# Attention into experts: where block 3's root, the gates, the shared matmuls and the late rows stand

## The reference, cut to what matters

```
x = x + tanh(g_xattn[1]) * _L1_xattn_ref(_layernorm(x), ctx, ...)
x = x + tanh(g_ffn[1])   * _L1_ffn_ref(_layernorm(x), gate, ...)

scores = sigmoid(xt @ gate.T)
_, sel = top_k(scores + expert_bias, 2)        # two experts for a row
xb = (xt[token] * score).astype(bfloat16)
for e in range(8):
    h = silu(xb @ w1e.T) * (xb @ w3e.T);  oe = h @ w2e.T     # added where expert == e
hs = silu(xt @ shared_w1.T) * (xt @ shared_w3.T)
out = hs @ shared_w2.T + the experts' rows
```

## Time and profile before

| what | value |
|---|---|
| time, median of 3 runs | 217.3 us (217.23 to 218.14) |
| the profiled execution's own time | 218.29 us |
| its span | 216.5 us, 3594 instructions |
| TensorE busy (matmuls) | 177.0 us, 82% |
| VectorE busy | 163.7 us, 76% |
| ScalarE busy | 106.9 us, 49% |
| POOL busy | 84.6 us, 39% |
| share of the chain that ended last: PE, DVE, ACT | 50%, 21%, 10% |

### The profile page before, as it was taken

One profiled execution on the slowest core, in us unless ns is written; L12 is line 12 of the kernel. 1 busy time (PEld: TensorE's weight loads), 2 busy tenths in 40 slices (PEclk: granted clock), 3 DMA queues, 4 the chain that ended last, 5 costly groups with the idle time before them and its releaser, 6 DMA issues.

```text
span 216.5 us, 3594 instructions
## 1 busy us (share of the span) xinstructions
PE 177.0 (82%) x1156; PEld 112.2 (52%) x1156; DVE 163.7 (76%) x465; ACT 106.9 (49%) x280; POOL 84.6 (39%) x123
## 2 busy tenths in 40 slices
PE   0369999999989989886789788888889568989992
PEld 0236555567555556543356465556666126744651
DVE  0798989995177899988688999999946942475854
ACT  2440243111423244641568798898877641554441
POOL 1385558016655550493032204222221396039000
PEclk9999999999999999997579999999999876999999
DMA  6989970000000000000000000000000245639862
GB/s 175 400 218 374 359 255 15 3 0 0 0 0 2 3 0 2 0 0 2 3 0 0 5 0 5 0 3 0 3 0 3 50 93 101 76 72 170 164 152 97
DMA packets 22625, 15.17 MB, mean 70 GB/s; under 512 B 17648, under 2 KB 21328, under 8 KB 22096
## 3 DMA queue, kind: packets, MB, share of 16 engines
q1 hardware_dynamic: 21968, 13.94, 24.3%
q10 hardware_dynamic: 640, 1.02, 1.3%
HBM read 9.68 MB, written 1.07 MB: 50 GB/s over the span
## 4 chain that ended last, share of the span: by engine, by line
PE 50%; DVE 21%; ACT 10%; issue 8%; DMA 6%; POOL 3%; SPq 0%; DVEq 0%
PE PS L1668 6%; PE PS L1334 5%; PE PS L1336 5%; PE PS L1335 5%; PE PS L1686 5%; DMA X<-x 4%; PE PS L1422 4%; PE PS L1398 3%; PE PS L1356 3%; ACT R L668 3%; ACT R L663 2%; PE PS L1498 2%; PE PS L1365 2%; DVE T_R L974 2%; POOL R L507 2%
## 5 line engine op out<-in xcount | busy, mean ns | idle before, releaser
L507 POOL TENSOR_SCALAR R<-QT,SM 128x256 bf16<-128x256 f32 x32 | 16.1, 520 | 15.6 <-DVE SM L1117 15.3
L1284 DVE TENSOR_TENSOR R<-R,PS 128x512 bf16<-128x512 f32 (+1 forms) x17 | 11.5, 683 | 13.7 <-PE PS L1668 7.3
L1036 DVE TENSOR_REDUCE SM<-PS 128x8 f32<-128x1024 f32 x16 | 18.8, 1213 | 3.7 <-PE PS L1498 2.5
L1512 PE MATMUL PS<-CON,R 128*128 128x128 f32 x128 | 19.0, 281 | 1.2 <-ACT R L668 1.2
L476 POOL TENSOR_TENSOR R<-R,CON 128x256 f32<-128x256 f32 x16 | 9.6, 620 | 25.3 <-PE PS L1498 16.2
L668 ACT ACTIVATE R<-PS 128x512 f32<-128x512 f32 x32 | 18.4, 601 | 1.2 <-PE PS L1512 1.0
L1686 PE MATMUL PS<-R 128*128 128x256 bf16 (+1 forms) x80 | 15.3, 318 | 4.3 <-DVE R L1284 4.0
L341 POOL TENSOR_TENSOR R<-CT 128x512 f32<-128x512 f32 x12 | 13.4, 1113 | 13.2 <-PE PS L1336 8.0
L1668 PE MATMUL PS<-R 128*128 128x512 bf16 x64 | 16.8, 382 | 0.1
L1512 PEld LDWEIGHTS PS<-CON,R 128*128 128x128 f32 x128 | 14.5, 143 | 3.5 <-issue 3.0
L790 ACT ACTIVATE R<-PS 128x512 f32<-128x512 f32 x17 | 10.1, 595 | 11.4 <-PE PS L1668 11.2
(11 more groups left out here) (155 smaller groups left out, 432.7 us busy)
## 6 DMA issues: line engine op xcount, KB each, us to landing
WST<-w SPq DMA_DIRECT2D x3, 1024.0 KB, 11.3
T_R<-lagged SPq DMA_DIRECT2D x2, 768.0 KB, 8.0
X<-x SPq DMA_DIRECT2D x2, 512.0 KB, 6.8
CT<-ctxr SPq DMA_DIRECT2D x1, 1024.0 KB, 7.4
y<-X SPq DMA_DIRECT2D x8, 128.0 KB, 1.8
WKV<-wkv SPq DMA_DIRECT2D x1, 512.0 KB, 9.8
WQP<-wqp ACTq DMA_DIRECT2D x1, 512.0 KB, 6.4
R<-sw SPq DMA_DIRECT2D x3, 128.0 KB, 4.4
```

The lines of the kernel that those rows point to most:

```text
L507: nc.gpsimd.tensor_scalar(XB[:, u % XS, j, :], MX[:, b, :], GG[:, b, e:e + 1], 1.0, ALU.mult, ALU.mult).then_inc(e_xb, 1)
L1036: V_.tensor_reduce(MX1[:, b % 2, 8 * c:8 * c + 8], S4[:, 8 * c:8 * c + 8, :], AX.X, ALU.max, negate=True).then_inc(a_mx, 1)
L1512: ins = TR(PS[:, 4 + k % 2, P * h:P * h + P], SS[:, b % 2, 4 * k + h, :], I)
```

## The change

The change alters only the order of calls, in six places.

- The root of block 3 (`m_rstd(NB - 5)`) moves from the tail into the loop's last turn on ScalarE, ahead of `o_y_(4)`. Two of the four blocks' logits are made in TensorE's last loop turn.
- Block 3's transpose, its copy and the other two blocks' logits come ahead of block 7's values.
- On VectorE the six steps of the gates come right behind block 6's division, ahead of block 7's; `finish(5)` goes behind `m_rows(4)`, into block 7's division.
- Both shared hidden matmuls of group 0 come ahead of block 7's `o_transpose`.
- The late rows: `m_rows`, transposes and copies of blocks 5 to 7, and `finish(7)` with its statistics, go behind units v = 0, 1 and 2; on POOL `late_rstd` of blocks 5 to 7 moves one or more units later.
- Group 1's gates come one unit later (GE_AT 4 to 5), and ROWS_AT with them.

```diff
@@ -46,7 +46,7 @@
 NS = 14
 RING = 6
 XS = 8
-ROWS_AT = {1: (4,), 2: (5,), 3: (6,), 4: (7,), 6: (8, 9), 7: (10,), 8: (11,), 9: (12, 13), 10: (14,), 11: (15,)}
+ROWS_AT = {1: (4,), 2: (5,), 3: (6,), 4: (7,), 7: (8, 9), 8: (10,), 9: (11, 12), 10: (13,), 11: (14,), 12: (15,)}
 
 D_AT, BIAS_AT = 0, NH0
 BV_AT = BIAS_AT + NR
@@ -366,7 +366,7 @@
 
             return PS[:, ((0, 1), (6, 0))[g][j // 2], DM * (j % 2):DM * (j % 2) + DM]
 
-        GE_AT = 4
+        GE_AT = 5
 
         LOG = 512 - GT * NE
         TC = [0, 2, 4, 10, NH0]
@@ -541,13 +541,14 @@
                 finish(b)
             late_rstd(GT)
             expert_rows(0)
-            late_rstd(GT + 1)
             expert_rows(1)
             expert_rows(2)
+            late_rstd(GT + 1)
+            expert_rows(3)
             late_rstd(GT + 2)
-            expert_rows(3)
+            expert_rows(4)
             late_rstd(GT + 3)
-            for u in range(4, NG * NE):
+            for u in range(5, NG * NE):
                 expert_rows(u)
 
         @block.scalar
@@ -764,6 +765,8 @@
                     o_ev_(s - 3)
                 if s + 3 < NB:
                     a_zq_(s + 3)
+                if s == NB - 1:
+                    m_rstd(NB - 5)
                 if s >= 3:
                     o_y_(s - 3)
                 if s >= 1:
@@ -791,29 +794,27 @@
 
 
             a_exp(NB - 1, 0)
-            m_rstd(NB - 5)
             o_q_(NB - 3)
             a_exp(NB - 1, 1)
+            m_zt_(NB - 5)
             a_exp(NB - 1, 2)
             o_ev_(NB - 3)
-            m_zt_(NB - 5)
             a_exp(NB - 1, 3)
+            m_ge_(0)
             o_q_(NB - 2)
             o_y_(NB - 3)
             o_pe_(NB - 1)
-            m_ge_(0)
             o_ev_(NB - 2)
+            last_rows(0)
+            nc.scalar.preload_act_table_set("silu_and_others")
             o_y_(NB - 2)
-            nc.scalar.preload_act_table_set("silu_and_others")
-            last_rows(0)
+            last_rows(1)
+            silu(0)
             o_q_(NB - 1)
-            last_rows(1)
+            last_rows(2)
             o_ev_(NB - 1)
-            silu(0)
+            m_zt_(NB - 4)
             o_y_(NB - 1)
-            m_zt_(NB - 4)
-            last_rows(2)
-            m_zt_(NB - 3)
             last_rows(3)
 
 
@@ -823,8 +824,8 @@
                     m_ge_(1)
                 for u in ROWS_AT.get(v, ()):
                     last_rows(u)
-                if v in (1, 2):
-                    m_zt_(NB - 3 + v)
+                if v in (1, 2, 3):
+                    m_zt_(NB - 4 + v)
             v = UNITS - 1
             act.wait_ge(e_h, 2 * v + 1)
             act.wait_ge(e_ht, v - 1)
@@ -1233,32 +1234,24 @@
             m_stats(NB - 4, 1)
             for k in range(3, 6):
                 o_norm(NB - 2, k)
+            for k in range(6):
+                m_gates(0, k)
+            third_rows(0)
+            o_norm(NB - 1, 0)
+            o_norm(NB - 1, 1)
+            m_rows(NB - 4)
+            o_norm(NB - 1, 2)
             finish(NB - 3)
-            m_rows(NB - 4)
-            for k in range(4):
-                m_gates(0, k)
-            o_norm(NB - 1, 0)
-            m_gates(0, 4)
-            o_norm(NB - 1, 1)
-            m_gates(0, 5)
-            o_norm(NB - 1, 2)
-            third_rows(0)
             for k in range(3, 6):
                 o_norm(NB - 1, k)
             third_rows(1)
             m_stats(NB - 3, 0)
+            third_rows(2)
+            m_stats(NB - 3, 1)
             finish(NB - 2)
-            m_stats(NB - 3, 1)
             m_stats(NB - 2, 0)
+            third_rows(3)
             m_stats(NB - 2, 1)
-            third_rows(2)
-            m_rows(NB - 3)
-            third_rows(3)
-            finish(NB - 1)
-            m_stats(NB - 1, 0)
-            m_stats(NB - 1, 1)
-            m_rows(NB - 2)
-            m_rows(NB - 1)
 
 
             for v in range(UNITS):
@@ -1282,6 +1275,13 @@
                     dve.wait_ge(e_acc, v - 1)
                 dst = HT[:, v % 2, :] if e >= 1 else HST
                 V_.tensor_tensor(dst, HS[:, v % 2, :], PS[:, 3 + 2 * (v % 2), :], ALU.mult).then_inc(e_ht, 1)
+                if v == 0:
+                    m_rows(NB - 3)
+                    finish(NB - 1)
+                    m_stats(NB - 1, 0)
+                    m_stats(NB - 1, 1)
+                if v in (1, 2):
+                    m_rows(NB - 3 + v)
 
                 if v == GE_AT + 1:
                     for k in range(4):
@@ -1635,6 +1635,8 @@
                     a_turn(s - 1, 3)
                 if s + 1 < NB:
                     a_scores(s + 1)
+                if s == NB - 1:
+                    m_logits(0, 0, 2)
                 if s >= 3:
                     o_transpose(s - 3)
                 if s >= 1:
@@ -1698,25 +1700,23 @@
             a_turn(NB - 1, 0)
             a_turn(NB - 1, 1)
             o_rows(NB - 2)
-            m_logits(0, 0, GT - 1)
+            m_transpose(NB - 5)
+            a_turn(NB - 1, 2)
             o_transpose(NB - 3)
-            a_turn(NB - 1, 2)
-            m_transpose(NB - 5)
             a_turn(NB - 1, 3)
+            m_logits(0, 2, GT)
             o_project(NB - 3)
             for k in (0, 2, 1, 3):
                 a_values(NB - 1, k)
-            m_logits(0, GT - 1, GT)
             o_transpose(NB - 2)
             o_rows(NB - 1)
             o_project(NB - 2)
             e_hidden(0, 0)
+            e_hidden(0, 1)
             o_transpose(NB - 1)
+            m_transpose(NB - 4)
             o_project(NB - 1)
-            e_hidden(0, 1)
-            m_transpose(NB - 4)
             e_hidden(1, 0)
-            m_transpose(NB - 3)
             e_hidden(1, 1)
             for v in range(1, UNITS + 1):
                 if v < UNITS:
@@ -1724,8 +1724,8 @@
                         e_hidden(v, 0)
                         e_hidden(v, 1)
                 e_out(v - 1)
-                if v in (1, 2):
-                    m_transpose(NB - 3 + v)
+                if v in (1, 2, 3):
+                    m_transpose(NB - 4 + v)
                 if v == GE_AT - 1:
                     m_logits(1, 0, GT)
```

## The result

| kernel | runs | median, us | lowest to highest |
|---|---|---|---|
| before | 4 | 217.72 | 217.23 to 218.56 |
| changed | 4 | 208.74 | 207.89 to 209.84 |

What follows compares the result with a forecast made beforehand. TensorE was the engine to follow, with three large holes and low clock behind two. Terms 6.8 + 1.36 + 1.7 - 0.55 + 0.45 = 9.75, less 0.35, gave 9.4 us: 217.3 to 207.9 us, 8-in-10 range 206.7 to 211.0.

Steps and rivals of the forecast that it cites:

- hole 3: TensorE idle 1.29 us ahead of e_out(7), from group 1's gates; moving them one unit later gains 1.7 us.
- unit 8: Expert 8's rows on POOL come late behind the moved gates, DMA landing 190.4, wanted 189.85: gives back 0.55 us.
- The loop: Last turn: eight logit matmuls ahead of o_transpose(4) cost 0 to 0.1 us; block 3's root makes o_y(4) 0.15 late.
- Up to the shared matmuls: Tail: block 3's root no longer holds back m_rows(3); hidden(0,0) starts at 166.45 against 166.69.
- Gates and division: VectorE starts gates at 163.95; block 7's scaling ends 5.1 us later, at 169.0 instead of 170.2.
- hole 1: TensorE idle 2.13 us ahead of block 7's output transposes (170.70), low clock behind it; both predicted gone.
- First product: VectorE's first product of hidden rows starts at 171.8; e_out(0) at about 172.6 against 179.40, 6.8 us earlier.
- (a): Rival: TensorE's clock falls once more between 169.9 and 172.6, +1.7 us and more; 209.6 to 210.5, chance 0.17.
- (d): Rival, slower: clock at 1.2 GHz from the shared matmuls (166.45) on, all units at double time; some 219, chance 0.03.
- (b): Rival: the gates' hole only moves, to late rows of unit 8 and unit 5 or 6; 209.4, chance 0.14.
- (c): Rival: VectorE's queue is longer, stretched by POOL writing rows; product 0 at 173.5, 209, chance 0.10.
- (e): Rival: m_transpose(3)'s chain ends last, gates start at 166.5 as before, only 5 us won; 212.3, chance 0.04.

Runs made afterwards that it cites:

- r6: The changed kernel with block 3's root (Ln, Exp) back in the tail behind exp(7,0): 209.44 us, 0.9655 of before.
- r5: The changed kernel with m_rows of blocks 5 to 7, finish(7) and its statistics back ahead of product 0 on VectorE: 215.34 us, 0.9940 of before.
- r3: The changed kernel with block 7's output transposes and projection back between the two shared hidden halves: 211.2 us, 0.9714 of before.
- r9: The kernel before with 8 and 10 unused fp32 matmuls in TensorE's holes ahead of block 7's output transposes and e_out(0): 216.53 us, 0.9977 of before.
- r1: The changed kernel run again without an edit: 209.42 us, 0.9619 of before.
- r2: The changed kernel with group 1's gates back at their old unit (GE_AT 4, old ROWS_AT): 210.59 us, 0.9677 of before.
- r12: The kernel before with only group 1's gates one unit later (GE_AT 5, new ROWS_AT): 216.4 us, 0.9958 of before.
- r7: The kernel before with 16 and 22 unused fp32 matmuls in TensorE's holes ahead of block 7's output transposes and e_out(0): 218.14 us, 1.0049 of before.

## Why the prediction was right

By its own terms, in the profiled executions, all times from TensorE's timeline:

| term of the sum | predicted, us | measured, us | from |
|---|---|---|---|
| e_out(0) earlier | 6.8 | 6.65 | 179.40, 172.75 |
| e_out(0) to hidden(5) | 1.36 | 1.20 | 9.29, 8.09 |
| hidden(5) to hidden(9), hole 3 | 1.7 | 1.19 | 6.92, 5.73 |
| hidden(9) to hidden(11), unit 8 | -0.1 | -0.60 | 6.93, 7.53 |
| hidden(11) to the end | 0 | 0.06 | 13.96, 13.90 |
| taken off for unit 8's landing | -0.35 | in the -0.60 | |
| sum | 9.4 | 8.5 | 216.5, 208.0 |

The mechanism held in each of the four large terms, and three sizes were off. The 9.46 us of the prediction are one: they take e_out(0)'s start from the timeline and hidden(5)'s (188.86) from the chain, which puts the same matmuls 0.17 us later than the timeline does (188.69). The two others are hole 3 and unit 8, below.

- *The loop.* o_project(4) at 158.16 and o_y(4) at 158.69, 0.06 later than before, where I had taken 0.15. Nothing was lost to the eight logit matmuls, as the hole of 0.87 at that place had said.
- *Up to the shared matmuls.* They start at 166.00; predicted 166.45. The last four logits ran at 162.38, where I had 162.8, so the replay was late by 0.4 already there. The root's part is 0.76 us (r6), all of the earlier start against before.
- *Gates and division.* First step 163.68 (163.95), last 165.64, ahead of block 7's division. The scaling ends at 169.54, where I had 169.0: from the first gate step 5.86 us for 5.1, the largest miss of the replay. In it stand m_rows(4), which takes 0.58 us for 0.41, and finish(5), with POOL writing rows beside them from 165.93; no run tells whether POOL is the reason. TensorE did not wait for it, as both shared halves lasted to 169.5; of the 2.13 us of hole 1, 0.44 stayed.
- *First product.* At 172.04 (171.8); e_out(0) at 172.75 (172.6) behind a hole of 0.70 (0.7), and 1.99 us long (1.75). That it comes so close is in part luck: VectorE needed 8.36 us from the first gate step to the product, where I had 7.87, and the gates were 0.27 early. r5 shows that this term hangs on the late rows, r3 that it hangs on the shared matmuls' place too, and r9 that in the old order it did not hang on the clock behind hole 1.
- *Hole 3.* The mechanism was right: the gates' wait is the same 1.72 us and is covered. The term came out as 1.19 because hidden(6) came 0.50 late, a wait for a DMA (0.34) that r1 doesn't have.
- *Unit 8* is the mis-sized term: I had 0.55 lost, it was a wait of 0.89. The chain of waits in the changed kernel shows the parts:

```profile
188.06 0.05 POOL R L507
188.10 3.35 DMA R<-R
```

  POOL began at 186.96 instead of 186.2. That is 0.76 later, of which hidden(9) shared 0.62 (186.57 for 185.95). Then it took 1.10 for the first unit's rows, where I had taken the mean of fifteen, 0.95: the first pass alone lasts 0.64 us, as it does in the trace of before (at 193.00), and the median one 0.48. The landing of 3.35 was as predicted. A mean over a long run was the wrong row for its first unit.

*The rivals.* (a), the clock falling once more, is out: 1.00 from 160 to 192 us in the windows, behind holes of 0.44, 0.24 and 0.70. What (a) and (d) say of the trace of before, two low stretches, each behind a hole of over 2 us, misses a third: the clock is at 0.50 from 101 to 110 us as well, behind no such hole (last section), and the chances given for the clock were not worked out with it. (b), the gates' hole only moves: r2 and r12 show that the move gains 1.3 and 0.9 us net of unit 8's wait; but the half of (b) that unit 8 gives back more than I took was true. (c), product 0 at 173.5: it came at 172.04, though VectorE's queue was longer than I thought, by 0.5 us. (d) and (e) are out, by the clock and by the gates at 163.68. The rule on the table load (2.66 us by the Trainium skill, ScalarE: Activation LUTs, "What ACT_TABLE_LOAD costs") would have had e_out(0) at 173.1. In the changed kernel's timeline of ScalarE the load and its neighbours are:

```profile
165.87 0.51 ACT L786 ACTIVATE R<-QT,SM 128x256 bf16<-128x256 f32 x1 [0.35 <-DVE SM L1118]
166.39 1.28 ACT L809 ACT_TABLE_LOAD   x1
167.69 0.47 ACT L688 ACTIVATE T_R<-PS,SM 128x256 f32<-128x256 f32 x1
```

From the end of the one ACTIVATE (166.38) to the start of the next (167.69) it is 1.31 us, with work ready on both sides. The load itself is as long there as the Trainium skill gives it (1.28 us), but the trace shows no drain of 1.38 us beside it, and the sum did well to go by the row.

*The parts do not add up.* Taken back singly they cost 6.7 (late rows), 2.8 (shared matmuls), 2.0 (gates; 1.3 timed) and 0.7 (root): 12.2 in the traces, against 9.0 for all together (66.3 to 57.3, before and r1). The late rows and the shared matmuls both end in product 0, so part of the price of each hangs on the other; the shared matmuls' move in the old order was not run by itself.

Open: the timed gain beyond the profiled one. The medians differ by 9.0 us and the two profiled executions by 8.5; that is within the scatter. And what makes a landing of 4.4 to 4.9 us, which comes now and then; as before and r7 have one too (4.4 and 4.9), it is not the new order.

## What to carry to other kernels

Look at what stands ahead of the first product of a new stage in each queue, and move behind it all that only later units need, statistics and roots above all: taking that one move back cost 7 of 9 us. A hole's low clock is worth filling or avoiding only where the work behind it ends last; check that for each hole before spending anything on it: in the old order here it cost nothing behind hole 1 and 1.5 us behind hole 2. When a wait can't be taken away, put it where another engine has a long piece to do, and give the DMA behind it a unit more of lead.
